# Mixture of experts and state space in one part of a decoder: the experts' sum moved into the state-space steps

## The reference

```
shared = silu(xt @ sg_w.T) * (xt @ su_w.T) @ sd_w.T          # every row
probs  = sigmoid(xt @ router_w.T + routing_bias)             # 8 experts
topk_p, topk_idx = top_k(probs, 2); topk_p /= sum(topk_p)
h = silu(xt @ wg[e].T) * (xt @ wu[e].T); y_e = h @ wd[e].T   # for the chosen e
x = layernorm(x + shared + sum_e topk_p[e] * y_e)

z, xBC, dt = split(x @ in_proj_w.T)                          # 512, 768, 8 columns
xBC = silu(causal conv of 4 taps over rows (xBC) + conv_b); x_part, B, C = split(xBC)
dt = softplus(dt + dt_bias); A = -exp(A_log)
state = state * exp(A dt) + (x_part dt) B;  y = C . state     # row after row, 8 heads of 64
y = (y + x_part D) * silu(z); y = y * rsqrt(mean(y*y) + eps) * norm_w
x = layernorm(x + y @ out_proj_w.T)
```

## Time and profile before

| | us |
|---|---|
| median of three runs | 3015.48 |
| the profiled execution | 3013.87 |
| its span | 3010.7 |
| PE busy in the span | 2506.7 (83%) |
| DVE busy | 1911.4 (63%) |
| ACT busy | 1434.2 (48%) |
| POOL busy | 1591.5 (53%) |
| mean granted clock of TensorE | 0.911 |

### The profile page before, as it was taken

One profiled execution on the slowest core, in us unless ns is written; L12 is line 12 of the kernel. 1 busy time (PEld: TensorE's weight loads), 2 busy tenths in 40 slices (PEclk: granted clock), 3 DMA queues, 4 the chain that ended last, 5 costly groups with the idle time before them and its releaser, 6 DMA issues. The chain is left out here.

```text
span 3010.7 us, 68328 instructions
## 1 busy us (share of the span) xinstructions
PE 2506.7 (83%) x25416; PEld 2101.6 (70%) x25416; DVE 1911.4 (63%) x3347; ACT 1434.2 (48%) x2243; POOL 1591.5 (53%) x1778
## 2 busy tenths in 40 slices
PE   5999999995799978999999802888877599996998
PEld 4676766764576757999999802777777477765897
DVE  2666666775478862436665565878887267774665
ACT  2566655653466652335555401555554255653332
POOL 3566655664354530776666583445444367763343
PEclk8899999998799996999999955989998699997999
DMA  7555655532777832246666473010000578762111
GB/s 167 128 136 142 148 130 133 137 92 67 189 201 200 206 87 84 92 157 205 205 218 223 163 211 106 19 32 21 31 28 22 145 192 219 197 157 70 53 52 46
DMA packets 253228, 384.90 MB, mean 128 GB/s; under 512 B 54624, under 2 KB 184416, under 8 KB 245472
## 3 DMA queue, kind: packets, MB, share of 16 engines
q1 hardware_dynamic: 232448, 302.85, 37.9%
q0 software_dynamic: 17376, 78.13, 7.8%
q10 hardware_dynamic: 3200, 1.05, 0.2%
HBM read 249.05 MB, written 142.08 MB: 130 GB/s over the span
## 5 line engine op out<-in xcount | busy, mean ns | idle before, releaser
L1225 ACT ACTIVATE self_probs<-self_score_ps 128x768 f32<-128x768 f32 x256 | 207.6, 811 | 216.1 <-PE self_score_ps L1127 213.1
L1433 POOL TENSOR_SCALAR_AFFINE_SELECT self_probs<-self_probs 128x512 f32<-128x512 f32 x256 | 167.7, 656 | 217.0 <-ACT self_probs L1225 214.4
L2079 POOL TENSOR_TENSOR moee_h_lo<-moee_h,moee_h_hi 128x512 fp32r<-128x512 f32 x110 | 149.8, 1362 | 208.7 <-ACT moee_h_hi L1846 207.8
L1354 DVE TENSOR_REDUCE self_neg_max<-self_max_ps 128x2 f32<-128x256 f32 x256 | 108.0, 422 | 226.5 <-PE self_max_ps L1113 225.3
L672 DVE TENSOR_REDUCE cross_neg_max<-cross_max_ps 128x4 f32<-128x1024 f32 x128 | 155.9, 1221 | 69.9 <-PE cross_max_ps L461 68.6
L1950 DVE TENSOR_TENSOR moee_in_lo<-moee_in_raw,moee_in_hi 128x2048 fp32r<-128x2048 f32 x40 | 91.7, 2293 | 134.0 <-ACT moee_in_hi L1814 102.3
L1355 DVE TENSOR_REDUCE self_neg_max<-self_max_ps 128x2 f32<-128x512 f32 x256 | 174.2, 681 | 0.0
L589 ACT ACTIVATE cross_probs<-cross_score_ps 128x1024 f32<-128x1024 f32 x128 | 131.1, 1024 | 89.3 <-PE cross_score_ps L483 89.0
L1846 ACT ACTIVATE moee_h_hi<-moee_h 128x512 fp32r<-128x512 f32 x110 | 69.6, 632 | 187.5 <-DVE moee_h L2001 187.5
L3032 POOL TENSOR_TENSOR ffn_g_lo<-ffn_g_full,ffn_g_hi 128x512 fp32r<-128x512 f32 x64 | 82.4, 1287 | 144.3 <-ACT ffn_g_hi L2933 144.3
L79 PE MATMUL moee_g_ps<-moee_x_hi,moee_in_hi 128*128 128x256 f32 x440 | 131.9, 300 | 25.3 <-DVE moee_x_lo L1989 21.1
(11 more groups left out here) (475 smaller groups left out, 9932.2 us busy)
## 6 DMA issues: line engine op xcount, KB each, us to landing
self_q<-self_q_split SPq DMA_DIRECT2D x48, 512.0 KB, 3.2
self_q_raw<-self_q SPq DMA_DIRECT2D x32, 768.0 KB, 7.8
cross_stacks<-cross_qk SPq DMA_DIRECT2D x64, 384.0 KB, 6.9
causal_stacks<-causal_qk SPq DMA_DIRECT2D x64, 384.0 KB, 7.2
moe_y_tiles<-moee_y SPq DMA_DIRECT2D x55, 256.0 KB, 3.2
x_tiles<-zeros SPq DMA_DIRECT2D x16, 624.0 KB, 4.6
moee_x_t<-x_tiles SPq DMA_DIRECT2D x39, 256.0 KB, 3.2
cross_qk<-cross_k_split SPq DMA_DIRECT2D x16, 512.0 KB
```

The source lines that it names most:

```text
L1225: nc.scalar.activation(probs[g % 4][:, a, :, P:], score_ps[:, :, P:], ACT.Exp, scale=HD ** -0.5).then_inc(prob_ready, 1)
L1433: pool.affine_select(diagonal, diagonal, [[0, 2], [0, 2], [1, P]], ALU.is_ge, zero, base=0, channel_multiplier=-1).then_inc(prob_masked, 1)
L2079: pool.tensor_tensor(h_lo[p][f][:].rearrange("p j s -> p (j s)"), h[f][:], h_hi[p][f][:].bitcast(F32).rearrange("p j s -> p (j s)"), ALU.s ...
```

## The change

There are three parts to it.

The sum of the experts is no stage any more. `state_space` takes the experts' rows and gathers, sums and normalises a batch some steps before it is projected: the gather of batch n+7, the sums of n+5 and n+6 (both in odd steps n), the transposes of n+4. The residual of the expert sublayer is added where a shared tile's result is copied out of its bank. The state space projects two batches at once, with products of 512 columns: five of a pair's eleven units in an even step and six in an odd one. A chunk's taps are instructions over both batches (128x2x255 and so on). Exponents are multiplied in place (mat), the last normalisation is ACT's, and steps run from -7 to 16, all written out.

The stage of the tiles turns four batches ahead of tile 0 and the others between the products of tiles 0 to 2, into a tensor xT that stays and from which the shared tiles take their input. The routing follows from tile 2 to tile 6; the scatters start with tile 6, eight a tile, and h_lo of the shared tiles is DVE's.

A routed expert's first weights are split in two halves, one behind h and y, the other behind x_lo, and fetched in the second half of a tile.

```diff
-        scan = [m.sb(f"scan{i}", [P, KT, S]) for i in range(2)]
+        xT = m.sb("xT", [P, B, KT * S])
...
+        AHEAD = 4
+        BETWEEN = [(t, f, name) for t in range(3) for f in range(PAIRS) for name in "guy"
+                   if (t or name != "y") and (t, f, name) < (2, 0, "v")]
+        BETWEEN = dict(zip(sorted(BETWEEN, key=lambda k: (k[0], k[1], "guy".index(k[2]))), range(AHEAD, B)))
+        scan_ps = [xT_ps, y_ps[1]]
...
-            for b in range(SCANS):
+            def scan(st, f, name):
+                b = scan_at(st, f, name)
+                if b is not None:
+                    scan_batch(b)
+                    logits(b - 1)
+                    if b == B - 1:
+                        logits(b)
+            for b in range(AHEAD):
                 scan_batch(b)
                 if b:
                     logits(b - 1)
-            logits(SCANS - 1)
...
-                if (t, f) == (0, 0):
+                if (t, f) == (2, 1):
+                    add_biases()
+                if (t, f) == (3, 0):
+                    score_experts()
                     choose(0)
...
-                if (t, f) == (3, 0):
+                if (t, f) == (6, 0):
                     name_tiles(found["end"])
...
             def body(st):
                 p = st.parity(0)
-                if fresh(st, 1):
-                    lower_in(buffer(st, 1), sets(st, 1))
                 for f in range(PAIRS):
...
+                    if f == 1 and fresh(st, 1):
+                        lower_in(buffer(st, 1), sets(st, 1), 1)
                     if st.has(0):
...
                         dve.tensor_tensor(h[f][:], u_ps[f][:], silu[f][:], ALU.mult).then_inc(h_ready, 1)
...
-                        dve.tensor_copy(y[p][:].rearrange("p q d -> p (q d)"), y_ps[p][:]).then_inc(y_kept, 1)
+                        if shared(st, -2):
+                            c = QT * st.at(-2)
+                            kept = dve.tensor_tensor(y[p][:], y_ps[p][:].rearrange("p (q d) -> p q d", d=D),
+                                                     x_tok[:, c:c + QT, :], ALU.add)
...
+                    if f == 0 and fresh(st, 1):
+                        lower_in(buffer(st, 1), sets(st, 1), 0)
...
                         route(st.at(0), f)
+                        dve.wait_ge(hhi_ready, n + 1)
...
+                        dve.tensor_tensor(h_lo[p][f][:].rearrange("p j s -> p (j s)"), h[f][:],
+                                          h_hi[p][f][:].bitcast(F32).rearrange("p j s -> p (j s)"),
+                                          ALU.subtract).then_inc(shared_hlo_ready, 1)
...
-            FIRST, POINTS = 3, 6
+            FIRST, POINTS = 6, 8
...
             def body(st):
                 p = st.parity(0)
-                if fresh(st, 2) or fresh(st, 1):
-                    fetch(st)
                 for f in range(PAIRS):
-                    if st.has(0):
+                    if f == 1 and (fresh(st, 2) or fresh(st, 1)):
+                        fetch(st)
+                    if fresh(st):
...
-def combine(nc, stage, x_in, x_out, y_tiles, slot, weight, routed_loaded):
...
+    UNITS = ("B", "C", "x0", "x1", "x2", "dt", "x3", "z0", "z1", "z2", "z3")
+    TAPPED = ("B", "C", "x0", "x1", "x2", "x3")
...
+    STEPS = range(-7, B + 1)
...
+        def unit(n, i):
+            jp = n // 2 + 1
+            k = 5 * (n % 2) + i
+            return (jp, UNITS[k], len(UNITS) * jp + k) if 0 <= jp < PAIRS else None
...
+            def sum_experts(b):
+                p, i = b % 3, b % 8
...
+                for q in range(QT):
+                    c = b * QT + q
+                    dve.scalar_tensor_tensor(y_shared[p][:, q, :], y_routed[p][:, 0, q, :], weight[0][:, c:c + 1],
+                                             y_shared[p][:, q, :], ALU.mult, ALU.add).then_inc(part_ready, 1)
...
+                moments(b, x[i], c_stats, c_mv[b % 2], c_var[b % 2], c_low[b % 2], cstat_ready, cmean_ready, ceps_ready)
...
+            for n in STEPS:
+                now, late, soon = real(n), real(n - 1), real(n + 1)
+                even = n % 2 == 0
                 if now:
-                    dve.wait_ge(g_done, n)
...
+                    masked_products(n)
+                    tail_rows(n)
+                    matrices(dve, n, 0, low_mat_ready)
+                if even:
+                    taps(n, 0)
+                else:
+                    time_steps(n)
...
+                if soon:
+                    high_terms(n + 1)
+                if even:
+                    if soon:
+                        scaled_rows(n + 1)
+                    taps(n, 3)
...
+                else:
+                    if real(n + 5):
+                        sum_experts(n + 5)
...
+                if not even:
+                    if soon:
+                        scaled_rows(n + 1)
+                    if real(n + 6):
+                        sum_experts(n + 6)
...
+            for n in STEPS:
+                now, late, soon = real(n), real(n - 1), real(n + 1)
+                even = n % 2 == 0
+                if now:
+                    matrices(pool, n, 1, high_mat_ready)
+                    matrices(pool, n, 3, high_mat_ready)
...
+                if soon:
+                    low_terms(n + 1)
+                if late:
+                    scale_y(n - 1)
+                if real(n + 7):
+                    gather(n + 7)
+                if n == -6:
+                    split_weights()
```

More of the change, by code:

```diff
@@ L2350, in mix @@
                         rows, cols = slice(half * HP, (half + 1) * HP), slice(h * HP, (h + 1) * HP)
[L2351 removed]
+                        out = y_ps[blk][rows, f * S:(f + 1) * S]
                         kw = dict(skip_group_check=True)
[L2353 to L2354 removed]
@@ new lines, in skip_terms @@
+            def skip_terms(n, blk):
+                if blk == 0 and n:
+                    dve.wait_ge(yhi_ready, n)
+                    dve.wait_ge(sq_ready, n)
+                    dve.wait_ge(ylo_ready, n)
+                dve.wait_ge(ssm_done, 2 * n + blk + 1)
+                for i in range(2):
+                    f = 2 * blk + i
+                    last = dve.scalar_tensor_tensor(yz[:, f, :], cols_of(xs[:, n // 2 % 2, f, :], n), dcol[:, f:f + 1],
+                                                    y_ps[blk][:, i * S:(i + 1) * S], ALU.mult, ALU.add)
+                last.then_inc(yd_ready, 1)
@@ L3043, in decoder @@
     rows = B * S
-    mid = [nc.dram_tensor(f"mid{i}", (rows, D), F32, kind="Internal").ap() for i in range(4)]
+    mid = [nc.dram_tensor(f"mid{i}", (rows, D), F32, kind="Internal").ap() for i in range(3)]
     x_tiles = nc.dram_tensor("x_tiles", (ALL_TILES * TILE, D), F32, kind="Internal").ap()
```

1101 lines of the change are left out of this document (601 added, 500 removed).

## The result

The changed kernel takes 2977.88 us (median of four runs, 2975.34 to 2979.18), against 3014.41 of the kernel before beside it: ratio 0.989, interval 0.9869 to 0.9911. It is faster, by 36.5 us (34.8 between the two profiles) and not by the 136 that were forecast; the range began at 2825 and ended at 2930.

What follows compares the result with a forecast made beforehand. It took DVE and a ring of exponents to bound the loop, POOL's scatters the routed tiles' start, and PE's waits the routed tiles. 3013.9 - 107.9 + 3.1 - 13 - 18 = 2878 us, range 2825 to 2930.

Steps and rivals of the forecast that it cites:

- The sum's stage goes, 107.9: Stage that sums the experts: its 107.9 us leave the span, its work moves into the state space.
- 73 us into the state space: State space, start: first masked product at 73 us instead of 43.2, bounds 60 and 90.
- DVE's work of 25.3 a step: State-space loop: DVE's busy time per step goes from 24.5 to 25.3 us, experts' sum included.
- case (c): Rival, state-space loop: collisions and late gathers lengthen steps to 31.5 and 28, +35 us, 2913; chance 0.13.
- 3.6 idle: 28.9 a step: State-space loop: DVE idles 3.6 us a step, so steps with sums take 28.9, bounds 25.3 and 31.5.
- a ring of 10.3 us: State-space loop: PE's products from the first exponents on, plus ACT's exponent, take 10.3 us against 6.9 of DVE's work there.
- case (d): Rival, state-space loop: PE's clock stays at the lower level throughout, kernel slower than before at 3098; chance 0.03.
- The recorded sign: State-space loop: a step over 30 us says that the lock between DVE and POOL costs more than 1.5.
- PE's wait for xdt: Start of state-space steps: PE's idling of up to 5.3 us, 66.4 in 14 times, goes in even steps.
- the four steps forecast at 25.7: State-space loop from step 10 on: batches are already summed, so the 3.3 us is gone and steps take 25.7.
- The term -18: Routed tiles: split weights make x_lo ready, 7 of 24.7 us idle remain, -18, bounds -22 and 0.
- The tiles' start: From tile 0 to the first routed input: scatters, POOL's chain, set its turning at 1319 instead of 1332.1, -13 us.

Runs made afterwards that it cites:

- keep_busy: Changed kernel with 30 products of 256 columns that nobody reads put into PE's wait in each state-space step; ratio to the kernel before 0.9793.
- x_lo_first: Changed kernel with DVE's x_lo of batch n+4 in odd steps ahead of the second experts' sum; ratio to the kernel before 0.9841.
- out_early: Changed kernel with ACT's out_hi of a routed tile directly behind the second silu, ahead of the wait for h; ratio to the kernel before 0.9779.
- both_orders: Changed kernel with x_lo ahead of the second sum and the squares behind the second projection; ratio to the kernel before 0.9811.
- late_busy: Changed kernel with the squares late and 28 unneeded products a step; ratio to the kernel before 0.9791.
- best3: Changed kernel with out_hi early, routing packed with scatters from tile 5, squares late and 28 unneeded products a step; 2917.3 us, ratio to the kernel before 0.967.
- after_again: The changed kernel unaltered, run once more in the last job; 2987.95 us, ratio to the kernel before 0.993.

## Why the prediction was wrong

**Right.** The sum's stage goes, 107.9. The first masked product was forecast 73 us into the state space and came at 77.4. DVE's work of 25.3 a step: 102.27 / 4 = 25.6, with the held instructions where they were expected. What POOL holds up is now what stands beside it in the new order, 2.96 for two weighted sums (0.87 elsewhere):

```profile
2056.92 1.88 DVE L2604 TENSOR_SCALAR ssm_var<-ssm_mv 128x2 f32<-128x2 f32 x1
2068.09 2.96 DVE L2612 SCALAR_TENSOR_TENSOR ssm_y_shared<-ssm_y_routed,moek_weight,ssm_y_shared 128x256 f32<-128x256 f32 x2
...
2068.14 2.63 POOL L2845 TENSOR_TENSOR ssm_y_lo<-ssm_yz,ssm_y_hi 128x1024 fp32r<-128x1024 f32 x1 [2.01 <-ACT ssm_y_hi L2517]
```

These are of the kernel after, DVE and POOL. The late gathers of case (c) didn't occur: in the loop they took 0.94 to 1.11 each, but for one of 1.83.

**The step that failed, in the loop:** "I take 3.6 idle: 28.9 a step", and the sentence before it, a ring of 10.3 us in which every product of PE was priced at the upper level. The earlier trace rows had shown the contrary at this very place: after 4.59 us of waiting the product took 0.80 instead of 0.40. I used that row for the unlikely case (d) alone, in which the clock stays down for the whole loop, and not for the first 12 us of each step. DVE's idle time was (135.71 - 102.27) / 4 = 8.4 a step, not 3.6, and a step with sums took 33.9, not 28.9; 3.5 of the 4.8 us of idle time too much is the clock, by keep_busy. The rest, 1.3 a step, is left open. The recorded sign, that a step over 30 means a dearer lock, would have misled: DVE's busy time, which holds what the lock costs, was 25.6 as forecast, and the step was long all the same. I had said that PE's wait for xdt would go in even steps and named the ring as what is late next; late next was x_lo, which the change puts behind a sum (x_lo_first), and in the odd steps the squares' input and the tail, from ACT. Of the four steps forecast at 25.7, the first, step 10, took 33.1: its projection still waited 5.06 for an x_lo behind the last sum, which stands in step 9. The others took 27.3, 27.8 and 25.6, and the last step 22.2 instead of 16.

**The step that failed, in the routed tiles:** "with in_lo in two halves behind h and x_lo, x_lo is ready; what is late next is the weight itself". The first half was right. Late next was out_lo, which I hadn't followed: ACT makes out_hi last in a tile, DVE's out_lo comes behind it, and POOL's h_lo holds it. out_early shows it. The term -18 was +8; with the one line moved it is -26.

**The tiles' start:** the mechanism was right and sizes were off: tile 0 at 1154.9 and not 1152.2, of which PE's first product is 2.9 later; the first scatter at 1236.4 and not 1231.5; 1.32 a scatter and not 1.27; 7.6 us from the last scatter's end to the first routed input and not 6. Together 9.4.

## What to carry to other kernels

When work is moved off one engine into a loop, price what follows an engine's gap at the clock that the trace grants there, not at the loop's mean. After splitting the operation that was late, follow the next consumer in program order on every engine: here one conversion at the end of ACT's list decided between 8 us lost and 26 gained. And look at what is put ahead of a value that another engine waits for at a step's boundary, for a gap there is paid twice, as waiting and as a slow start.

## What the runs showed of the hardware that I had not expected

- Products that nobody needs, put into PE's waits, shortened the loop by 37.6 us (467.7 to 430.1), with the granted clock up from 0.81 to 0.94 in the four steps shown.
- A tiny DVE instruction with one input, 128x2, took 1.88 us beside a POOL product, and 0.16 in the step before it. The Trainium skill, "SBUF — State Buffer", section "SBUF: two separate sides", has DVE's fast modes take the shared port pair, as well as two inputs from SBUF, each held for a whole instruction. The 1.88 fits that: it ended at 2058.80, and POOL's two products rhs_lo, from 2055.02 on, at 2058.78. Whether this instruction ran in a fast mode the trace doesn't tell.
- The same shared tiles took longer in three of the jobs (keep_busy to both_orders, late_busy to best3, and the last) than in the others: the tiles' start is 10 to 15 us longer where the routing is as in the change, 21 to 27 where it is packed. There PE shows 25 to 31 gaps up to the first routed input, most of 0.2 to 0.8 us, inside runs of products and with no releaser, 16 to 19 us in all; the kernel after shows one, of 3.1. And PE then reaches the first routed input without a wait for the scatters, so that packing them earlier brings nothing. PE alone was ready 173.5 - 13.8 = 159.7 us behind tile 0 in the kernel after and 185.3 in after_again: 26 us, of which the gaps seen are only about half. The lines below are of after_again and then of after, 1155 to 1320 (groups by line; the last part is idle time and its releaser):

```profile
L81 PE MATMUL moee_u_ps<-moee_x_hi,moee_in_lo 128*128 128x256 f32 x115 | 33.2, 289 | 2.0 <-issue 2.0
```

```profile
L81 PE MATMUL moee_u_ps<-moee_x_hi,moee_in_lo 128*128 128x256 f32 x124 | 35.6, 287 | 0.0
```

The kernel before took the same time in those jobs as in the others (medians of 3010.8 to 3014.4 over all jobs). What PE waits for there isn't shown by these profiles, and it was not tried.
